# A four-layer graph network on one core: a turned copy of x with columns 8 bytes apart, a residual product in another bank, and two sums earlier in VectorE's order

## The reference, cut to what matters

```python
edge_index = jnp.stack([src, dst])                      # 50000 edges, dst sorted, 100000 nodes x 128
x = _layernorm(x + relu(concat([x, max_diff(x)]) @ L0_W + L0_b))       # max over a node's edges of x[dst] - x[src]
x = _layernorm(x + L1(x, ...))     # L1: xx = silu(x @ lin_W.T + lin_b)
                                   #     h1, h2 = silu(...xx...), h = [h1, h2] @ cat_W.T + cat_b + xx
                                   #     three times: h = silu(h @ lins_W[i].T + lins_b[i]) + h
                                   #     norm over all nodes, final_W
x = _layernorm(x + L2(x, ...))     # graph convolution with degrees
x = _layernorm(x + L3(x, ...))     # graph convolution with edge weights, layer norm
```

## Time and profile before

| | |
|---|---|
| runs | 5658.59 us, median of 3 (5655.28 to 5660.55) |
| the profiled execution | span 5689.4 us, with no other time shown of it |
| stage `nodes01` | from about 70 to 2130 us of the span |
| busy in the span | PE 81%, DVE 76%, ACT 64%, POOL 73% |
| DMA, mean | 213 GB/s; queue q1 (SyncE's) 59.1% of the 16 engines, q0 (GpSimd's) 10.2% |

### The profile page before, as it was taken

The page is one execution under the profiler, slowest core; times in us unless marked ns, Lnnn a source line. Parts: engine busy times, 40 slices in busy tenths (PEclk is TensorE's granted clock), DMA queues, the critical chain, the costliest instruction groups (busy, mean ns, idle before and its releaser), DMA issues. The chain is left out here.

```text
span 5689.4 us, 82998 instructions
## 1 busy us (share of the span) xinstructions
PE 4597.0 (81%) x18558; PEld 2788.2 (49%) x18558; DVE 4328.5 (76%) x8746; ACT 3650.3 (64%) x9127; POOL 4126.8 (73%) x4125
## 2 busy tenths in 40 slices
PE   6999999999999997899999999999777656662000
PEld 4555555555555543344444467777555434441000
DVE  7777777777777765688888789999788864447776
ACT  3666666666666663566666668888688863336665
POOL 5777777777777767677777357777777767777777
PEclk9999999999999998999999999999855556665555
DMA  5666666666666654677777689999888866665443
GB/s 163 183 186 179 177 181 186 186 176 179 182 186 181 176 153 121 204 203 207 203 207 203 186 296 363 363 365 366 294 286 283 281 212 223 220 218 173 138 134 105
DMA packets 699928, 1213.28 MB, mean 213 GB/s; under 512 B 146894, under 2 KB 366472, under 8 KB 699686
## 3 DMA queue, kind: packets, MB, share of 16 engines
q1 hardware_dynamic: 594038, 1059.81, 59.1%
q0 software_dynamic: 100352, 149.23, 10.2%
q10 hardware_dynamic: 5296, 1.73, 0.1%
HBM read 648.60 MB, written 438.76 MB: 191 GB/s over the span
## 5 line engine op out<-in xcount | busy, mean ns | idle before, releaser
L839 ACT ACTIVATE p_s<-p_ps,cols 128x512 f32<-128x512 f32 x588 | 403.9, 687 | 597.1 <-PE p_ps L793 400.9
L716 POOL DMA_INDIRECT p_xs<-in_x,src_cols x388 | 424.9, 1095 | 271.7 <-DVE p_r L898 182.4
L723 POOL DMA_INDIRECT home<-edge_row_cols,scatter_cols x392 | 442.9, 1130 | 119.3 <-issue 119.0
L191 POOL DMA_INDIRECT u_rows<-t_rows,home_cols x392 | 406.9, 1038 | 145.5 <-issue 118.2
L198 POOL DMA_INDIRECT out<-u_res,scatter_cols x392 | 407.7, 1040 | 121.8 <-issue 118.4
L1188 POOL DMA_INDIRECT ring_rows<-t_rows,home_cols x384 | 408.5, 1064 | 119.3 <-issue 88.6
L191 POOL DMA_INDIRECT ring_rows<-t_rows,home_cols x400 | 399.1, 998 | 126.3 <-issue 117.1
L716 POOL DMA_INDIRECT p_xd<-in_x,dst_cols x388 | 397.3, 1024 | 107.5 <-issue 97.1
L1197 POOL DMA_INDIRECT home_cols<-home,src_cols x376 | 368.6, 980 | 145.1 <-issue 86.0
L787 PEld LDWEIGHTS p_ps<-w_swapped,p_xT 128*128 128x128 f32 x1568 | 400.1, 331 | 121.3 <-issue 82.0
L787 PE MATMUL p_ps<-w_swapped,p_xT 128*128 128x128 f32 x1568 | 389.2, 393 | 39.2 <-DMA p_xT<-p_xt 32.1
(11 more groups left out here) (304 smaller groups left out, 14037.8 us busy)
## 6 DMA issues: line engine op xcount, KB each, us to landing
ring_rows<-in_x SPq DMA_DIRECT2D x98, 512.0 KB, 5.8
p_xT<-p_xt SPq DMA_DIRECT2D x392, 128.0 KB
t_rows<-p_o SPq DMA_DIRECT2D x98, 512.0 KB
p_x1T<-p_oT SPq DMA_DIRECT2D x392, 128.0 KB
hT<-ring_own SPq DMA_DIRECT2D x98, 512.0 KB
q_hn<-hT SPq DMA_DIRECT2D x98, 512.0 KB, 4.0
r_h<-hT SPq DMA_DIRECT2D x98, 512.0 KB
r_x<-t_rows SPq DMA_DIRECT2D x98, 512.0 KB
```

Of the source, the lines that this page charges most:

```text
L191: nc.gpsimd.indirect_dma_start(out=rows[:, j, :], out_offset=None, in_=table, in_offset=bass.IndirectOffsetOnAxis(ap=idx[:, j:j + 1], axis ...
L716: nc.gpsimd.indirect_dma_start(out=rows[:, j, :], out_offset=None, in_=a["x"], in_offset=bass.IndirectOffsetOnAxis(ap=idx[:, j:j + 1], axi ...
L723: nc.gpsimd.indirect_dma_start(out=tab["home"], out_offset=bass.IndirectOffsetOnAxis(ap=s["scat"][:, k:k + 1], axis=0), in_=s["at"][:, k:k ...
L839: nc.scalar.activation(act_out[i][:, :], flat(bank_r), ACT.Silu, bias=col(LS0 + i)).then_inc(r_act[i], 1)
```

## The change

Three edits, all in `nodes01`. The layout of the two tiles becomes (4 tiles, 32 columns, 2 blocks) at the end, so that the columns of one tile lie 2 floats (8 bytes) apart. In `xT` the tile index stands ahead of the group of 32 partitions, so each DMA now writes four pieces of 64 floats in each partition. The first residual product goes to `bank_t`, and its wait for `r_act[2]` goes to the second one; in odd steps it waits for `xd_copied`. In VectorE's step the sum `residual(0)` comes ahead of `turn_x`, and the edge bias (L972) and the sum L978 come ahead of the turn of `oe` and the scan.

```diff
-        x_turned, xT = sb("p_xt", [P, 2, 4, 32, 2, G]), sb("p_xT", [P, 2, 4, 32, 2, G])
+        x_turned, xT = sb("p_xt", [P, 2, 4, G, 32, 2]), sb("p_xT", [P, 2, G, 4, 32, 2])
@@ sync
-                    swap_groups(sp, xT[:, q % 2], x_turned[:, q % 2], xT_in[q % 2])
+                    swap_groups(sp, xT[:, q % 2].rearrange("p j a i h -> p a j (i h)"), x_turned[:, q % 2], xT_in[q % 2])
@@ tensor
                     pe.wait_ge(r0_ready, n.b + 1)
-                    after(pe, r_act[2], n.b)
-                    nc.tensor.matmul(flat(bank_r), s["lins"][:, 0, :], hs[0][:, n.of(2), :],
+                    if e.live(EB) and not even:
+                        pe.wait_ge(xd_copied, e.b + 1)
+                    nc.tensor.matmul(flat(bank_t), s["lins"][:, 0, :], hs[0][:, n.of(2), :],
                                      start=True, stop=True).then_inc(r_done[0], 1)
...
-                        i = nc.tensor.matmul(bank_o[:, j, :], xT[:, q.of(2), :, :, t.slot % 2, j].rearrange("p a i -> p (a i)"), first["w0"][:, :],
+                        i = nc.tensor.matmul(bank_o[:, j, :], xT[:, q.of(2), j, :, :, t.slot % 2].rearrange("p a i -> p (a i)"), first["w0"][:, :],
...
                     pe.wait_ge(r_added[0], n.b + 1)
+                    after(pe, r_act[2], n.b)
                     nc.tensor.matmul(flat(bank_r), s["lins"][:, 1, :], hs[1][:, n.of(2), :],
@@ scalar
-                nc.scalar.activation(act_out[i][:, :], flat(bank_r), ACT.Silu, bias=col(LS0 + i)).then_inc(r_act[i], 1)
+                nc.scalar.activation(act_out[i][:, :], flat(bank_r if i else bank_t), ACT.Silu,
+                                     bias=col(LS0 + i)).then_inc(r_act[i], 1)
@@ vector
-                turn_squares(nc, x_turned[:, q.of(2), :, :, n.slot % 2, :].rearrange("p c i j -> p c j i"),
-                             x[:, n.of(8)]).then_inc(x_squared, 1)
+                turn_squares(nc, x_turned[:, q.of(2), :, :, :, n.slot % 2], x[:, n.of(8)]).then_inc(x_squared, 1)
...
+                n = t.back(8)
+                if n.live(NB):
+                    residual(0, n)
                 n = t.back(-X_AHEAD)
                 if n.live(NB):
                     turn_x(n)
-                n = t.back(8)
-                if n.live(NB):
-                    residual(0, n)
...
                     residual(1, n)
+                if not even and e.live(EB):
+                    dve.wait_ge(e_product, e.b + 1)
+                    after(dve, e_applied, e.b - 1)
+                    nc.vector.tensor_tensor(ve[:, e.of(2)], bank_e[:, :, :], to4(s["b0"]), ALU.add).then_inc(e_biased, 1)
+                n = t.back(7)
+                if n.live(NB):
+                    dve.wait_ge(cat_done, n.b + 1)
+                    after(dve, r_done[0], n.b - 1)
+                    after(dve, r_added[0], n.b - 1)
+                    nc.vector.scalar_tensor_tensor(hs[0][:, n.of(2), :], flat(bank_h), col(CAT_B), xx[:, n.of(2), :],
+                                                   ALU.add, ALU.add).then_inc(r0_ready, 1)
                 n = t.pair().back(BEHIND + 2)
                 if even and n.live(EB):
...
-                if not even and e.live(EB):
-                    dve.wait_ge(e_product, e.b + 1)
...
```

## The result

The changed kernel takes 5714.97 us (median of 4 runs, 5703.03 to 5716.64). The kernel before took 5659.57 us beside it (4 runs, 5655.28 to 5668.46). The ratio is 1.0091 [1.0077, 1.0105]: 55 us slower. The forecast was a gain of 49 us, so its sign is wrong, though the time lies in the range. The changed kernel's profiled execution has a span of 5714.9 us and so agrees with its runs; the one before lay 30 us above its own.

The account below looks back on a forecast made before the run. It took the loop through the scan and SyncE's list as the bound: landing 13.6 + 0.96 - 0.75 = 13.8, then 0.1 + 6.6, period 20.5 against 21.0. Times 98 pairs: -49 us, 5640 profiled or 5610 by median; range 5520 to 5800.

Parts of the forecast that it names:

- The bound: In `nodes01`, the loop scan, SyncE's list, `xT` landing, product, next scan sets the new period, 20.5 us against 21.0.
- C: Rival: SyncE's burst shrinks until TensorE and GpSimd set the pace; 19.2 us per pair, -176 us, 5482; chance 0.12.
- its floor of 19.2 us for GpSimd: GpSimd's work per pair in `nodes01`: it would need 20.7 - 1.5 = 19.2 us.
- Weight load and turn: `xT` weight load on TensorE falls from 331 to 192 ns; VectorE's turn of x from 1084 to 704 ns.
- D: Rival: the new columns load no faster, L787 keeps 1.79 us; period 21.4, +39 us, 5698; chance 0.10.
- The packets: `xT` DMAs write 2048 pieces of 256 bytes at 19.0 ns instead of 512 of 1 KB; landing 0.96 us later.
- B: Rival: small `xT` packets cost like 1 KB ones; period 23.9, +290 us, 5945; chance 0.12.
- The landing: From the scan's end until the `xT` DMAs land: 13.6 + 0.96 - 0.75 = 13.8 us, product 0.1 later.
- The relief from the scatters: GpSimd's last scatter ends 0.9 us after the next scan, 1.2 earlier, easing SyncE's burst; landing 0.75 us sooner.
- from the landing to the scan: Product 0.9 us sooner, L978 adds 0.65 and waits for cat; 6.6 us, as long as before.
- The base: The 49 us gain was taken from the profiled span 5689 (5640) and from the runs' median 5658.6 (5610).
- A: Rival: no relief of SyncE's burst from GpSimd's scatters; landing 14.5, period 21.2 to 21.3, +24 us, 5683; chance 0.24.

Follow-up runs that it names:

- x3: Changed kernel with SyncE's penalty-row load and store of the squares of `oe` moved behind the `xT` DMAs; 5451.5 us, 0.9622 to the kernel before.
- x5: Changed kernel with only the sum of cat's bias (L978) put back behind the scan; 5669.14 us, 0.995 to the kernel before.
- x2: Kernel before with the new layout alone (8-byte columns, 256-byte pieces), VectorE's order as before; 5648.14 us, 0.9964 to the kernel before.
- x1: Kernel before with only the bank and the earlier sums, columns still 32 bytes apart, 1 KB pieces; 5728.44 us, 1.0112 to the kernel before.
- x9: Changed kernel with only SyncE's penalty-row load moved behind the `xT` DMAs; 5459.97 us, 0.9643 to the kernel before.
- x7: Kernel before with the new layout and SyncE's penalty load and squares store behind the `xT` DMAs, order and banks old; 5487.9 us, 0.9635.
- x10: Changed kernel plus three extra 384-column products on TensorE ahead of its `xT` wait in even steps; 5688.64 us, 1.0039 to the kernel before.
- x11: Kernel before with only the first residual product in `bank_t` and its waits; 5661.14 us, 0.9997 to the kernel before.
- x8: Changed kernel with SyncE's penalty load and squares store behind the `xT` DMAs, columns 16 bytes apart, 512-byte pieces; 5611.39 us, 0.985 to the kernel before.

## Why the prediction was wrong, point by point

- **The bound: right.** The loop scan, SyncE's list, landing, product, scan sets the period. TensorE waits 2.0 us per pair (forecast about 2), in all 47 even steps; x3 shows it by removal. C did not come, and its floor of 19.2 us for GpSimd was wrong too: x3 runs at 18.64, near the 18.4 put down for TensorE.
- **Weight load and turn: right.** 201 and 709 ns against the 192 and 704 taken; D is false.
- **The packets: right in price, short in landing.** In 1032 to 1033 us of after nearly all packets are those of `xT`:

```profile
q1 hardware_dynamic: 1062, 0.26, 116.8%
```

  That is 1.168 x 16 / 1062 = 17.6 ns each (forecast 19.0), so B is false. SyncE's issue of the four DMAs took 2.73 us, 0.68 each, against 2.52; in the mean over the stage it took 3.15 against 2.54, a part of the pieces' price that the sum did not have. The landing, counted to the product's start, is 14.12 against 13.8 + 0.1 = 13.9.
- **The relief from the scatters: borne out as a link, not shown as a cause.** GpSimd's last scatter ended 0.6 us ahead of the scan's end in the pair followed above (timeline of after):

```profile
1000.31 1.00 POOL L723 DMA_INDIRECT home<-edge_row_cols,scatter_cols  x1 [0.30 <-issue]
...
1004.03 0.99 POOL L716 DMA_INDIRECT p_xs<-in_x,src_cols  x1 [2.73 <-DVE p_r L901]
```

  The landing of that pair was 13.28. Over the pairs of the stage the scatter ended on average 0.8 us ahead of the scan's end, where it ended 1.9 us after it in the kernel before; the forecast was 0.9 after. In the 32 pairs of after in which it ended 0.5 us or more ahead, the landing is 13.70; in the 22 in which it ended 0.5 us or more behind, it is 14.75. In x5 the same split gives 13.91 (21 pairs) and 15.6 (51 pairs), in x2 13.98 (13) and 15.2 (54); with the 1 KB pieces of x1 it is weaker, 13.47 and 13.89. This also fits the later landings of x2 and x5: there the scatter ended 1.3 and 1.1 us after the scan. So a part of what the rest wins comes back as a later landing. But no run moved the scatters alone, and the gathers move with them.
- **The step that failed: from the landing to the scan, "6.6. It is as long as before".** It is 7.16 us in the mean, 6.79 in the median. It was right only for a TensorE that does not wait: in x3 and x9, with the same order on VectorE and no wait for `xT`, the rest is 6.68 and 6.69. The text saw that L978 (now L966) delays the scan and has to wait for cat, and set its 0.65 us off against the 0.9 of the faster product. What it put at nothing is the slow stretch of TensorE behind its own wait of 2 us, which reaches the scan through that sum. Taken alone (x5 against after) the move costs 7.16 - 6.04 = 1.12 us per pair, and 6.68 - 5.79 = 0.89 where TensorE does not wait (x3 against x7, which lacks bank and residual sum too). Of the 0.56 us by which 7.16 exceeds 6.6, 0.36 go when TensorE is kept busy (7.16 - 6.80, x10), so they are the clock: the forecast had the 2 us of waiting of TensorE in it and did not ask what the granted clock does after such a wait. In the kernel before the scan needs only the transposes and not cat, so a slow cat did not reach the loop.
- **The base: 30 us that the sum could not place.** The periods were counted from a profiled execution that ran 30 us above the runs' median, and their difference was taken from the median. Between the profiled executions the sum closes: 0.22 us (landing) and 0.56 us (7.16 - 6.6) are 0.78 us, times 98 pairs 76 us, against 5715 - 5640 = 75. The other 30 us of 5715 - 5610 = 105 are this excess, which the runs of the changed kernel do not have under their profiled execution. It was not late landings for the most part, as far as x11 can tell, which is as fast as before and whose profiled execution has a span of 5651.0 us:

```profile
L968 DVE TENSOR_TENSOR_SCAN p_run<-p_pen,p_run,p_ps x97: 1230/1237/1277, 88.9 to 2090.8; 128x512 f32<-128x512 bf16 x97
```

  Of the 38 us by which before lay above it, 11 are in the stage (2102.1 - 2090.8) and 27 behind the last scan, in code that is the same in all kernels here. That part took 3557 to 3587 us in the profiled executions of this study, 3584 in the one of after. So against x11 about 40 us of the loss are in the stage; what makes the rest of the program 24 us longer there stays open.
- **A (5683) was the nearest rival,** in its period (21.2 to 21.3 against 21.28) and not in its cause: its 0.75 us sat in the landing, and the time was lost behind it.

## What to carry to other kernels

When an instruction is moved ahead of one that closes a loop between engines, it brings its own wait into the loop: count what it waits for, at the clock that the waiting engine will then have. A wait in an in-order DMA list costs what all DMAs behind it lose: moving the one load that waits behind the swaps took the changed kernel from 1.0091 to 0.9643, while with the old layout both moves gave 0.5%. Two bounds that lie close together hide each other's gain: test each removal together with the other one before it is given up.

## What the runs showed of the hardware

- **Weight loads (128x128 float32) by the columns' distance:** packed 192 ns, 8 bytes 196 to 207 (x3, x5), 16 bytes 325, 32 bytes 331. The Trainium skill, "SBUF — State Buffer", Specifications, has lines of 16 bytes and two hits per line for full speed; x8 agrees, with nearly the whole price due at 16 bytes.
- **Packets from SBUF to SBUF:** 256 bytes in 17.6 ns, 1 KB in 46. The Trainium skill, "DMA: Bandwidth & Descriptors", Specifications, has transfers under 512 bytes read, modified and written; here the small ones take about 1.5 times as long per byte, and no run shows whether that is the reason.
- **The granted clock after a short wait:** 2.29 us of waiting in a full stretch were followed by 0.50, and products of 1.78 us for 1.02. Three useless products ahead of the wait gave 0.5% back.
- **One loop's length moves another's:** with shorter products the product from `xT` started later (14.28 to 14.79 us, x2). It goes with GpSimd's scatters, which then end later against the scan; the cause stays open.
- **A layout with both 8-byte columns and 1 KB pieces** wasn't tried.
